# Graph layer on one core: the first group's adjacency work moves into the layer-norm front, and the branches to the general path are joined into one at the end

## The reference, cut to what matters

```python
h = jnp.maximum(_layernorm(x, axis=-1), 0.0)
# layer 0: attention over the neighbours
node_att = softmax(h @ node_w, axis=0)
e = (h @ edge_w) @ (h @ edge_w).T
edge_att = softmax(where(adj > 0, e, -9e15), axis=1)
x = x + (adj * (node_att * edge_att)) @ (h @ weight) + bias
# layer 1: hyperbolic mean over the neighbours
h = jnp.maximum(_layernorm(x, axis=-1), 0.0)
XW  = mobius_matvec(W, h)                       # row-wise, with artanh and tanh
AXW = weighted_midpoint_lincomb(adj, XW)        # needs adj @ (gamma * XW), adj @ (gamma - 1)
x = x + expmap0(relu(logmap0(AXW)))
```

## Time and profile before

| what | value |
|---|---|
| median of the 3 runs | 1020.68 us (1014.89 to 1023.57) |
| the profiled execution's own time | 1012.71 us |
| its span in the trace | 1011.1 us |
| mean granted TensorE clock | 0.739 of full speed |
| PE busy | 535.5 us (53%) |
| DVE busy | 452.9 us (45%) |
| POOL busy | 380.7 us (38%) |
| ACT busy | 338.6 us (33%) |

### The profile page before, as it was taken

One profiled execution on the slowest core, in us unless ns is written; L12 is line 12 of the kernel. 1 busy time (PEld: TensorE's weight loads), 2 busy tenths in 40 slices (PEclk: granted clock), 3 DMA queues, 4 the chain that ended last, 5 costly groups with the idle time before them and its releaser, 6 DMA issues.

```text
span 1011.1 us, 12998 instructions
## 1 busy us (share of the span) xinstructions
PE 535.5 (53%) x3644; PEld 433.0 (43%) x3644; DVE 452.9 (45%) x1815; ACT 338.6 (33%) x705; POOL 380.7 (38%) x447
## 2 busy tenths in 40 slices
PE   4675506377665677656665776830326336443540
PEld 3563305266545566455655664620214224332430
DVE  3762644557545565554743417651004223221327
ACT  2557613344534244344312126760002101110126
POOL 3351257330534515153353100001763565556610
PEclk8997657587676877768887796875658677776875
DMA  8428766555475455743121100014431332333315
GB/s 322 130 84 319 302 252 217 166 198 183 158 268 187 136 191 178 255 156 136 42 82 44 32 1 1 1 47 135 107 94 37 78 96 72 75 79 90 79 26 166
DMA packets 43911, 131.99 MB, mean 131 GB/s; under 512 B 7120, under 2 KB 24400, under 8 KB 35664
## 3 DMA queue, kind: packets, MB, share of 16 engines
q1 hardware_dynamic: 27344, 84.88, 23.0%
q0 software_dynamic: 16512, 46.49, 17.0%
HBM read 118.69 MB, written 12.65 MB: 130 GB/s over the span
## 4 chain that ended last, share of the span: by engine, by line
PE 28%; another core or an unknown queue 21%; issue 18%; DVE 13%; ACT 9%; DMA 3%; DVEq 3%; ACTq 2%; POOL 2%; SPq 0%; POOLq 0%; PEldq 0%
PE bank L1232 7%; PE bank L683 6%; PE bank L640 4%; PE bank L732 4%; PE bank L227 4%; DVE fs L896 2%; ACT work L523 2%; DMA front<-in_x 1%; ACT work L1245 1%; DVE gx L1596 1%; ACT work L574 1%; ACT front L200 1%; ACT work L1249 1%; DVE front L864 1%
## 5 line engine op out<-in xcount | busy, mean ns | idle before, releaser
L589 POOL DMA_INDIRECT work<-table_h,work x160 | 156.9, 981 | 229.8 <-PE bank L683 128.5
L1179 POOL DMA_INDIRECT work<-table_y,work x160 | 154.0, 963 | 109.3 <-issue 48.2
L1232 PE MATMUL bank<-work 128*128 128x257 f32 x320 | 104.3, 487 | 162.6 <-ACT work L1245 117.1
L523 ACT ACTIVATE work<-work 128x2048 bf16<-128x2048 f32 x64 | 121.8, 1904 | 102.5 <-remote 79.1
L1232 PEld LDWEIGHTS bank<-work 128*128 128x128 f32 x320 | 75.3, 245 | 182.1 <-ACT work L1245 106.0
L683 PE MATMUL bank<-work 128*128 128x128 f32 x640 | 111.5, 346 | 41.8 <-issue 21.1
L683 PEld LDWEIGHTS bank<-work 128*128 128x128 f32 x640 | 104.9, 256 | 43.3 <-issue 25.1
L1196 DVE TENSOR_SCALAR work<-work 128x640 bf16<-128x640 f16 x32 | 12.8, 402 | 191.6 <-remote 130.4
L896 DVE CUSTOM_DVE_ANT_0 fs<-work,bank 128x256 f32<-128x256 f32 x160 | 58.7, 418 | 84.5 <-PE bank L732 41.9
L732 PE MATMUL bank<-gx,front 128*128 128x256 bf16 (+1 forms) x480 | 68.0, 294 | 37.5 <-issue 25.2
L640 PE MATMUL bank<-work 128*128 128x256 bf16 x512 | 83.7, 328 | 7.0 <-ACT work L523 6.2
(11 more groups left out here) (231 smaller groups left out, 920.4 us busy)
## 6 DMA issues: line engine op xcount, KB each, us to landing
work<-in_adj SPq DMA_DIRECT2D x64, 1024.0 KB
table_y<-work SPq DMA_DIRECT2D x8, 520.0 KB, 6.2
front<-in_x SPq DMA_DIRECT2D x8, 512.0 KB, 4.6
table_h<-front SPq DMA_DIRECT2D x8, 512.0 KB, 3.2
front<-in_x POOLq DMA_DIRECT2D x8, 512.0 KB, 5.0
out<-gx SPq DMA_DIRECT2D x8, 512.0 KB, 3.0
work<-table_h,work POOLq DMA_INDIRECT x160
work<-table_y,work POOLq DMA_INDIRECT x160
```

The costliest lines, as they stand in the source:

```text
L523: a.activation(abf[:, h, :], adu[:, b % 2, h, :], ACT.Copy, accum_out=cnt[:, k, b, h:h + 1]).then_inc(L["conv"], 1)
L589: p.indirect_dma_start(gat[:, k, n, :], None, table_h, bass.IndirectOffsetOnAxis(ix[:, k, n:n + 1], 0)) \
L1179: p.indirect_dma_start(gt2[:, k, n, :], None, table_y, bass.IndirectOffsetOnAxis(ix2[:, k, n:n + 1], 0)) \
L1232: last = t.matmul(bank[4 + b % 2][:, 0:DY], otf[:, b % 2, q, :], gt2[:, k, b * TILES + q, 0:DY], start=(q == 0), stop=(q == TILES - 1))
```

## The change

It has two parts.

**The adjacency stage of group 0 beside the first front.** `staged` can now be written out without a loop (`rolled=False`), can start at a later step (`begun`), and can call a function `beside(n)` at the end of each step n. The first front is written out, and beside its steps ACT converts half n-1 of group 0 (steps 1 to 8), PE packs half n-2 (steps 2 to 9, in banks 6 and 7), DVE takes the keys of blocks 0 and 1 at step 6 and of blocks 2 and 3 at step 9, and makes the edge list at step 10; ACT converts the first two halves of group 1 at step 10. SP loads block 0 ahead of three weights, and blocks 2 to 5 in halves, one after each store of the front. The fast path starts at its step 1. `key` lies in `fs` now, since its old place is in use by the front.

**One decision at the end.** The two pairs of barriers with the branch between are gone. All engines run parts 2 to 5 straight through, and the waits that the barriers gave are put in by name (POOL waits for `tyo`, the landing of `table_y`, before the second gather; ACT waits for `proj` before the second front). After its own last work each engine waits for the flag, loads it, and runs the whole general path if it is set.

```diff
-        def staged(eng, body):
+        def staged(eng, body, begun=0, rolled=True, beside=None):
             def step(n):
                 stage = lambda d: (n - d, (n - d) % 2) if 0 <= n - d < NG else None
                 body(stage(0), stage(1), stage(2), stage(3))
-            for n in range(3):
+                if beside:
+                    beside(n)
+            if not rolled:
+                for n in range(begun, NG + 3):
+                    step(n)
+                return
+            for n in range(begun, 3):
                 step(n)
...
-        key = spare[:, 0:2 * KEY].rearrange("p (a b) -> p a b", a=2)
+        assert KEY == D
+        key = fs[:, 0:2, :]
...
-            p.drain()
+            p.drain().then_inc(s_const, 1)
+
+        def load_block(e, n, k, halves=range(UNITS)):
+            for h in halves:
+                if isinstance(n, int) and n < 2:
+                    e.dma_start(adu[:, k, h, :], adj[n * P:(n + 1) * P, h * UW:(h + 1) * UW]).then_inc(L["adj"][k][h], 16)
+                else:
+                    e.wait_ge(L["conv"], UNITS * (n - 2) + h + 1)
+                    e.dma_start(adu[:, k, h, :], adj[bass.ds(n * P, P), h * UW:(h + 1) * UW]).then_inc(L["adj"][k][h], 16)
+
+        EARLY = GB + 2
+
+        def early_half(e, v):
+            n = 2 + v // UNITS
+            load_block(e, n, n % 2, (v % UNITS,))
...
+        def unit_conv(a, g, k, u):
+            b, h = u // UNITS, u % UNITS
+            a.wait_ge(L["adj"][b % 2][h], 16 * (2 * g + b // 2 + 1))
+            a.wait_ge(L["pack"], UNITS * GB * g + UNITS * b + h + 1)
+            a.activation(abf[:, h, :], adu[:, b % 2, h, :], ACT.Copy,
+                         accum_out=cnt[:, k, b, h:h + 1]).then_inc(L["conv"], 1)
+
+        def early_act(a):
+            def beside(n):
+                if 1 <= n <= UNITS * GB:
+                    unit_conv(a, 0, 0, n - 1)
+                if n == NG + 2:
+                    unit_conv(a, 1, 1, 0)
+                    unit_conv(a, 1, 1, 1)
+            return beside
...
-            staged(a, body)
+            staged(a, body, 1)
...
-            p.drain()
-
-        def general_if(eng, general=None, fast=None):
-
+            p.drain().then_inc(s_flag, 1)
+
+        def general_path(eng, *parts):
+
+            eng.wait_ge(s_flag, 1)
             f = eng.value_load(flag[0:1, 0:1], min_val=0, max_val=1)
             with eng.If(f > 0):
-                if general:
-                    general(eng)
+                for part in parts:
+                    barrier(eng)
+                    if part:
+                        part(eng)
                 eng.nop()
             with eng.Else():
-                if fast:
-                    fast(eng)
                 eng.nop()
...
+        def early_pe(t):
+            t.wait_ge(s_const, 1)
+            t.sem_inc(L["pack"], UNITS)
+
+            def beside(n):
+                if 2 <= n <= UNITS * GB + 1:
+                    unit_pack(t, 0, n - 2, (6, 7))
+            return beside
...
+        def early_dve(d):
+            d.sem_inc(L["key"], 2)
+
+            def beside(n):
+                if n == 6:
+                    keys(d, 0, 0, 0, (6, 7))
+                if n == NG + 1:
+                    keys(d, 0, 0, 1, (6, 7))
+                if n == NG + 2:
+                    edge_list(d, 0, 0, None)
+            return beside
...
             p.drain().then_inc(F["const"], 1)
+            p.wait_ge(bf.tyo, 16 * NG)
             with p.Fori(0, NG // 2) as j:
...
             load(1, 1)
+            load_block(e, 0, 0)
             e.dma_start(w0[:, :, :], weight.rearrange("(c p) d -> p c d", p=P)).then_inc(s_w2, 16)
...
-            with e.Fori(0, (NG - 2) // 2) as j:
-                for k in (0, 1):
-                    store(2 * j + k, k)
-                    load(2 * j + k + 2, k)
-            store(NG - 2, 0)
-            store(NG - 1, 1)
+            for g in range(NG):
+                store(g, g % 2)
+                if g + 2 < NG:
+                    load(g + 2, g % 2)
+                early_half(e, g)
+            for v in range(NG, UNITS * (EARLY - 2)):
+                early_half(e, v)
             fast_load(e)
-            barrier(e)
-            general_if(e, ga_sp)
-            barrier(e)
...
+            table_sp(e, bf)
+            out_sp(e, bf)
+            general_path(e, back_again, table, gm_sp, lambda e: out_sp(e, bf))
...
             fast_flag(p)
-            barrier(p)
-            general_if(p)
-            barrier(p)
-            p.memset(ys[:, :, :, D:DYP], 0.0)
-            p.drain().then_inc(s_ysz, 1)
-            barrier(p)
-            general_if(p, None, fm_pool)
-            barrier(p)
+            table_pool(p, bf)
+            fm_pool(p)
+            general_path(p, None, lambda p: table_pool(p, bf), None, None)
...
-            staged(a, first)
+            staged(a, first, rolled=False, beside=early_act(a))
             fast_act(a)
-            barrier(a)
-            general_if(a, ga_act)
-            barrier(a)
...
+            a.wait_ge(L["proj"], GB * NG + 2)
+            second_act(a, bf)
+            fm_act(a)
+            out_act(a, bf)
+            general_path(a, ga_act, lambda a: second_act(a, bf), gm_act, lambda a: out_act(a, bf))
```

More of the change, by code:

```diff
@@ L554, in body @@
                     aggregate(b)
-                for u in range(2 if ls else 0, UNITS * GB):
+                for u in range(2, UNITS * GB):
                     conv(u, wd)
@@ new lines, in out_dve, with front_pe, steps, body @@
+        def out_dve(d, B):
+            midpoint_dve(d)
+            d.drain().then_inc(B.u, 1)
+            for n in range(NB):
+                d.wait_ge(B.us, n + 1)
+                d.tensor_tensor(x1[:, n, :], nom[:, n, 0:D], x1[:, n, :], ALU.add).then_inc(B.o, 1)
+        def front_pe(f, rhs, n):
+            def steps(t):
+                def body(st, nm, tr, pd):
+                    if tr:
+                        front_transpose(t, f, *tr)
+                    if pd:
+                        front_product(t, f, rhs, n, *pd)
+                return body
+            return steps
```

353 lines of the change are left out of this document (175 added, 178 removed).

## The result

The changed kernel takes 989.22 us (median of four runs, 980.34 to 992.52), the kernel before 1017.98 in the same runs (1014.89 to 1023.57): ratio 0.9698, 95% interval 0.9613 to 0.9783. It is faster by 3.0%, where 1.9% was forecast. 989 lies at the very edge of the range of 988 to 1012 and outside the forecast's own 995 to 1010, and the forecast ratio of 0.981 lies outside the interval. The profiled execution of after is its fastest, 980.34 us with a span of 978.7; before it was 1011.1. So 32.4 us have to be found in the two traces, 3.6 more than between the medians.

What follows compares the result with a forecast made beforehand. No engine filled its part; waits counted: the first adjacency stage standing alone and two meetings. Gains 9.1 + 2.4 + 8.9 less 0.9 made 19.5 us, 1020.7 to 1001 us; own range 995 to 1010, with rivals 988 to 1012.

Steps and rivals of the forecast that it cites:

- Start, to the edges of group 0: Kernel start: front 8.4 us longer, separate adjacency stage gone, edges at 98.1 instead of 107.23; gain 9.1 us.
- First meeting: Between the flag's reduction and the second front's statistics: without barriers 0.2 us remain of 2.57; gain 2.4 us.
- Second front and second meeting: From table_y's landing to the first gather, 10.22 us: POOL's iota configuration moves early and barriers go; gain 8.9 us.
- End: After the last store: SP now loads the flag and branches there; 0.9 us lost.
- the exposed wait: Before the first edges: DVE, ready at 92.3, stands nearly 6 us for POOL's configuration (8.4) and reduction.
- The term for the keys: Front, step 6: PE's pack waits for DVE's first key, delaying DVE's next copy; 4.4 us longer.
- The other three: Additions to the front: ACT's eight conversions 1.0 us, PE packs in two low-clock steps 2.0, last pack 1.0.
- (a): Fast path: gives back the start's gain by waiting for loads; only 10.4 us gained, 1010.3; chance 0.14.
- (b): First front: every addition counts in full, 37.4 us instead of 8.4; 1030, slower; chance 0.05.
- the ring: First front's cycle of product, ACT copy, norm and DVE's last rest, 6.96 us a step, with short idle pieces beside it.
- (c): Second gather: POOL must configure again behind the landing; gain 2.1 instead of 8.9, 1008; chance 0.05.
- (d): Front: keys don't hold PE, configuration is short, PE's clock stays high; 27 us gained, 994; chance 0.12.

Runs made afterwards that it cites:

- h1: The changed kernel unaltered, run on a chip with holds: 983.11 us, ratio 0.9679 to the kernel before (1012.65 us).
- f2: The kernel before, unaltered, traced on a chip without holds: 818.99 us in a single run.
- f1: The changed kernel unaltered, on a chip without holds: 794.46 us, ratio 0.9716 to the kernel before (816.91 us).
- g1: The changed kernel unaltered, run again on a chip without holds: 792.14 us, ratio 0.9683 to the kernel before (817.61 us).
- f4: Changed kernel with DVE's negation put behind its first edges' masks and ACT's exponential behind two conversions: 789.96 us, ratio 0.9666 to the kernel before.
- e3: Changed kernel without its decision at the end, the general path left out: 794.04 us, ratio 0.9725 to the kernel before.
- e4: Changed kernel with the second gather's transfers waiting block by block, not for the whole group of twenty: 793.64 us, ratio 0.9713 to the kernel before.
- f3: Changed kernel with the first two blocks' keys on DVE at step 5 instead of 6: 793.27 us, ratio 0.9697 to the kernel before.
- g3: Changed kernel with keys block by block, negation and exponential moved later, and SP's flag load ahead of the output stage: 786.99 us, ratio 0.9637.
- g4: Changed kernel with SP loading the flag ahead of the output stage, only the branch left behind: 793.57 us in a single run.
- g2: Changed kernel with the first group's keys block by block at steps 4, 6, 8 and 9: 790.29 us, ratio 0.9661 to the kernel before.
- e2: Changed kernel with only the early adjacency stage; barriers and branches between stages kept, general path left out: 803.57 us, ratio 0.9832 to the kernel before.
- e1: Changed kernel with only the one decision at the end; first adjacency stage behind the front as before: 806.94 us, ratio 0.9886 to the kernel before.
- h2: Changed kernel with the second gather released block by block, on a chip with holds: 975.58 us, ratio 0.9622 to the kernel before.

## Why the prediction was off

The terms in the traces, in us saved: on the left the forecast, then four pairs of traces (before and after of the first result; before and h1; f2 and f1; f2 and g1). The first two pairs have holds. h1 is set against the first trace of the kernel before, since there is none of it from h1's chip.

| Term | Forecast | first | h1 | f1 | g1 |
|---|---|---|---|---|---|
| Start, to the edges of group 0 | 9.1 | 10.8 | 12.4 | 10.3 | 12.0 |
| Fast path, edges to flag | 0 | 0.5 | 5.6 | 5.1 | 4.1 |
| First meeting | 2.4 | 2.3 | 2.3 | 2.3 | 2.3 |
| Second front and second meeting | 8.9 | 8.0 | 8.7 | 7.3 | 7.5 |
| Second gather | 0 | 12.8 | -4.8 | 1.9 | 2.3 |
| End | -0.9 | -2.0 | -2.0 | -2.0 | -2.1 |
| Sum | 19.5 | 32.4 | 22.2 | 25.0 | 26.1 |

**What held.** The four forecast terms that the change touches add up to 19.1, 21.4, 17.9 and 19.7 us, against 19.5. The first meeting is right to 0.1. The second meeting itself gave 9.1 (10.22 to 1.08), and the second front lost 1.1. The mechanism of the start is as told: the configuration of POOL takes the place of the removed stage, DVE waits 4.3 us for it (the working had nearly 6, 3 to 8 were named), and PE stands behind DVE's first key. That the exposed wait was worth what it looks like is shown by f4's median, 4.5 us lower, and not by f4's trace.

**What was mis-sized inside the start.** The front became 4.5 us longer (f1) or 5.7 (first trace), not 8.4. The term for the keys was 4.4 and came out at 4.4. The other three (conversions 1.0, packs at a low clock 2.0, the last pack 1.0) came out at 0.1 together in f1, where the fourth product starts 0.04 later and the last `rest` follows the sixth product as it did; in the first trace the fourth product is 1.05 later, in g1 0.90 earlier. The cover in the earlier trace rows was enough for one conversion and one pack per step. Against that the configuration took 9.5 us where I took the mean of three, 8.4; in all sixteen traces this one reduction stands 9.3 to 11.1 us behind the split, and 9.3 to 10.1 in the thirteen with the early adjacency stage. The price of its own place, 10.3 in the prediction, was a little nearer than the 8.4; the rows of other places drew the mean down. The end costs twice the 0.9, 2.0 us, of which e3 gives 1.4 to 1.8 to the decision.

**The step that failed** is what I set to nothing: "the second gather, 279.5 us long, is not touched inside", and, from "Afterwards step 1 goes as before" on, a fast path of unchanged length. The sum had no term for a change of either stretch, and both changed although their work didn't.

The second gather was 12.8 us shorter in the first pair of traces, and over two executions of the changed kernel it scatters by 17.6 us where there are holds. So of the 32.4 us about 19 are the change's terms, and nearly all of the rest is a long gather drawn before and a short one after. This accounts for the pair of traces. The medians with holds, 28.8 and 29.5 us apart, are 9 to 10 us above the forecast 19.5 too, and for them the cause stays open: single draws should average out in them, and the intervals reach from 22 to 40 us.

Without holds the fast path is 3.7 to 5.1 us shorter than in f2 (f1, g1, e3, e4, f3, g3, g4; 6.6 in g2). Its first step does go as before: PE's third pack of the step starts 10.6 us behind the first edges in f1 and in f2. Two thirds of the difference lie in the last 80 us, from the last group's edges to the flag, where PE does the same 625 matmuls in both (first f2, then f1; PE's busy time, clock, DMA share, GB/s):

```profile
393.21:477.03 83.82, 68.68 (x625) 0.85 0.20 55
381.18:461.60 80.42, 65.82 (x625) 0.89 0.21 57
```

Counted so, this stretch is 80.3 to 80.5 us long at 0.89 in seven of the twelve traces without holds (e3, e4, f1, f3, g1, g2, g4), 83.1 to 83.8 at 0.85 or 0.86 in four (f2, e2, f4, g3), and 81.9 at 0.88 in e1. f4 is among the long ones, with a fast path of 370.3, which is where its 4.5 us went. So the missing 3 us go with PE's granted clock. What makes a version or an execution get the one or the other is not shown: there is one trace of each, and one of the kernel before without holds. A rival for the 5 us is that PE packs the first two halves of the next group ahead of the first edges now (16 matmuls, 3.0 us busy in f2, behind them); e2 packs early as well and has 369.0, e1 does not and has 368.8, so this alone doesn't shorten the stretch.

What the change is worth is seen best on the chips without holds, where the interval is narrow: 2.8% in one set of runs and 3.2% in the other, 22 to 26 us, more than my 19.5 by the fast path's 4 to 5 us and the gather's 2.

**The rivals.** (a) fell: the start's gain wasn't given back, the fast path got no longer (only f4's trace gives its further gain back). (b) fell: up to the fourth product, in step 6, the ring took 0.04 us of five conversions and four packs; only the first pair of keys it took in full and more, 4.4 for 2.7. (c) fell: the first gather starts 1.08 us behind the landing. (d), 994 with 27 us, was nearest in size (28.8), but not by what it named: the keys do hold PE for 4.95 us, the configuration was long (9.5), and the clock was no higher over the front's middle, 0.81 between 32 and 48 us for 0.89 before, and 0.51 for 0.76 between 55 and 62. That conversions and packs cost nearly nothing was in none of the rivals.

**The configuration against the page.** The Trainium skill, "GPSIMD Engine Reference", section "Instruction dispatch", gives about 6 us for the load ahead of the first call; here the reduction waited 9.5 us and the iota 6.95. For the reduction the rows were the better price.

## What to carry to other kernels

Take the price of a wait from the row at its own place, not from a mean over places: POOL's configuration is 9.3 to 11.1 us there in every trace. Beside a ring, count the longest piece that another engine waits for, here a DVE pair that PE needed in the middle of a step, and cut it or move it; the pieces that fitted the idle time cost 0.1 us here. Before a difference of two traces is explained, compare the stretches that the change leaves alone: where they differ by 10 us, their scatter is a term of the difference, and one trace of each kernel can't size the change. And ask of a gain at the start whether it is still there at the end of the next stage: f4's was not, in the one execution that was traced.

## What the runs showed of the hardware

The kernel before ran at 817 us on two chips and at 1013 us on another, and the changed kernel's busy times on ACT, DVE and POOL were the same in both cases. On the slower one PE, ACT and DVE stand still together while POOL issues indirect DMAs, often for 3 us and more: up to 13.5 us at a time in the second gather of the first trace after, up to 20.8 in h2, and up to 8.3 in the fast path. A single engine waits for longer (PE 22.2 us in the rows above). Where the trace names a releaser it often says "remote". Against traces without holds the second gather is 55 to 73 us longer and the fast path 125 to 131, of which 72 are common idle time and 37 PE's longer busy time at the lower granted clock (first trace after against f1; the rest wasn't taken apart). Why one chip has the holds is not known from these runs. They don't come from POOL's wait for the whole group (h2), and are absent in each of the twelve traces from the other two chips.
